# When the input of the next batch is loaded: third group of the batch two ahead, in a cross-attention and expert kernel

## What is computed

```python
def attention(ref_feat, sup_feat):              # ref_feat: layer-normed x, sup_feat: the context
    sup = relu(sup_feat @ W_fc.T + b_fc)
    ref = relu(ref_feat @ W_fc.T + b_fc)
    q = (ref @ W_q.T + b_q).reshape(bs, N1, 16, 16)
    k = (sup @ W_k.T + b_k).reshape(bs, -1, 16, 16)
    p = softmax(einsum('bqhd,bkhd->bhqk', q, k) / 4)
    out_h = einsum('bhqk,bkf->bhqf', p, sup)
    return ref + einsum('bhqf,hjf->bqhj', out_h, Wv).reshape(bs, N1, 256) + b_v

x = x + attention(layernorm(x), ctx)
x = x + ffn(layernorm(x))     # 8 experts, the top 2 of each row, and one base expert
```

## Time and profile before

| | us |
|---|---|
| median of 3 runs | 1425.2 (1423.08 to 1428.62) |
| time of the profiled execution | 1423.38 |
| its span, first to last instruction | 1421.6 |
| TensorE matmul (PE) busy | 1277.0 (90%) |
| TensorE weight load (PEld) busy | 885.3 (62%) |
| VectorE (DVE) busy | 742.6 (52%) |
| ScalarE (ACT) busy | 679.5 (48%) |
| GpSimd (POOL) busy | 240.9 (17%) |

### The profile page before, as it was taken

How to read it: one execution, slowest core, us unless ns; L and a number is a source line. 1 busy time by engine, 2 the same in 40 slices (tenths; PEclk the granted TensorE clock), 3 DMA queues, 4 the chain that set the end, 5 groups by cost and what they waited for, 6 DMA issues and landing times. The chain is left out here.

```text
span 1421.6 us, 24901 instructions
## 1 busy us (share of the span) xinstructions
PE 1277.0 (90%) x8100; PEld 885.3 (62%) x8101; DVE 742.6 (52%) x1550; ACT 679.5 (48%) x938; POOL 240.9 (17%) x236
## 2 busy tenths in 40 slices
PE   4779997997999799799979979999959999999992
PEld 4647775775777577577757757755525556666661
DVE  4246675675667566566756746777435112111113
ACT  4326664664756566466656646665622112222220
POOL 3311110211111111121111102000013601222110
PEclk9879999998999999899989989999979999999996
DMA  4663454455444446444444644453079501111115
GB/s 142 200 174 94 131 138 108 106 154 125 131 117 123 116 114 159 115 131 129 100 116 121 173 112 113 108 106 62 13 222 280 221 26 45 44 44 44 48 45 189
DMA packets 154927, 168.56 MB, mean 119 GB/s; under 512 B 69040, under 2 KB 140344, under 8 KB 154816
## 3 DMA queue, kind: packets, MB, share of 16 engines
q1 hardware_dynamic: 151360, 157.61, 42.1%
q0 software_dynamic: 3456, 9.47, 1.8%
HBM read 103.55 MB, written 63.31 MB: 117 GB/s over the span
## 5 line engine op out<-in xcount | busy, mean ns | idle before, releaser
L602 DVE TENSOR_REDUCE mx<-side 128x1 f32<-128x400 f32 (+1 forms) x1024 | 534.6, 568 | 142.6 <-PE side L454 130.6
L497 ACT ACTIVATE prob<-st 128x1024 f32<-128x1024 f32 (+1 forms) x416 | 411.6, 1022 | 215.8 <-PE st L475 215.4
L454 PE MATMUL side<-kst,qst 96*128 96x400 f32 (+1 forms) x1024 | 330.1, 382 | 3.8 <-DVE mx L602 2.4
L475 PE MATMUL st<-qst,kst 97*128 97x512 f32 (+1 forms) x832 | 268.8, 406 | 35.3 <-issue 28.8
L454 PEld LDWEIGHTS side<-kst,qst 96*128 96x128 f32 x1024 | 189.8, 190 | 115.6 <-issue 37.4
L487 PE MATMUL acc<-prob,v 128*32 128x256 f32 (+1 forms) x3328 | 207.6, 385 | 0.0
L475 PEld LDWEIGHTS st<-qst,kst 97*128 97x128 f32 (+1 forms) x832 | 149.3, 188 | 49.9 <-issue 32.1
L634 POOL TENSOR_TENSOR clo<-raw,chi 128x768 fp32r<-128x768 f32 (+1 forms) x32 | 60.8, 1900 | 517.3 <-ACT chi L528 517.3
L487 PEld LDWEIGHTS acc<-prob,v 128*32 128x32 f32 (+1 forms) x3328 | 95.7, 110 | 79.6 <-issue 23.3
L1432 DVE TENSOR_TENSOR hg<-sg,pu 128x512 f32<-128x512 f32 x40 | 27.5, 688 | 138.4 <-PE pu L1610 138.4
L640 POOL TENSOR_TENSOR flo<-fc,fhi 128x768 fp32r<-128x768 f32 (+1 forms) x32 | 61.0, 1907 | 217.0 <-ACT fhi L541 217.0
(11 more groups left out here) (162 smaller groups left out, 1431.9 us busy)
## 6 DMA issues: line engine op xcount, KB each, us to landing
kst<-parts_at SPq DMA_DIRECT2D x90, 400.2 KB, 5.5
parts_at<-parts SPq DMA_DIRECT2D x48, 384.0 KB, 5.1
v<-v_at SPq DMA_DIRECT2D x32, 408.0 KB
raw<-ctx_t SPq DMA_DIRECT2D x24, 384.0 KB, 3.3
v_at<-vst SPq DMA_DIRECT2D x32, 272.0 KB
wall<-gate_up SPq DMA_DIRECT2D x8, 1024.0 KB, 14.1
parts_at<-parts SPq DMA_DIRECT2D x16, 449.0 KB, 2.8
qst<-q_at SPq DMA_DIRECT2D x192, 32.0 KB, 5.8
```

The costliest lines, as they stand in the source:

```text
L454: pe.matmul(side[u.bank][:, 0:w], t.qst[0:96, pair, col * P:(col + 1) * P], t.kst[0:96, pair, o:o + w], start=True, stop=True).then_inc(si ...
L475: mm = pe.matmul(into[0:rows, i * 2 * NQ:(i + 1) * 2 * NQ], t.kst[0:97, GP * g + i, s * P:s * P + rows], t.qst[0:97, GP * g + i, :], start ...
L497: act.activation(prob[0:rows, s, :], st[(KT * g + s) % 2][0:rows, :], ACT.Exp, scale=float(DH) ** -0.5).then_inc(exp_done, 1)
L602: dve.tensor_reduce(mx[:, hq, r:r + 1], side[u.bank][:, 0:RANGES[r][1]], AX.X, ALU.max)\
```

## The change

`sp_load_x` moves. `x[1]` is now issued once before the batches, behind the last stores of the prologue and ahead of the first row of maxima. In the body, `x[b + 2]` is issued in group 2 of batch `b`, if there is such a batch, in place of `x[b + 1]` in group 0. The wait is now for the `xres` of the same batch's group 1. `x[1]` to `x[7]` are loaded once each, 256 KB a load, before and after the change; `x[0]` is loaded in the setup either way. Nothing else in the program differs.

```diff
                     if c == len(CHUNKS) - 1:
                         sp_load_values(sp, 0, 0)
+                sp_load_x(sp, 1, before_unit(("xres", 0, 0)))
                 sp_max_row(sp, before_unit(("tm", 0, 0)), 0)
 
                 def body(b, at):
...
                             sp_load_group(sp, *behind(b, g, 2))
                         if last + 1 < PHASES:
                             sp_load_values(sp, *behind(b, g, 1))
-                        if g == 0 and at + 1 < B:
-                            sp_load_x(sp, b + 1, resid_unit(b, at))
+                        if g == 2 and at + 2 < B:
+                            sp_load_x(sp, b + 2, body_unit(b, at, 1, "xres", 0))
                         if active(at, g, "p"):
```

## The result

The changed kernel takes 1390.28 us (median of 4 runs, 1389.01 to 1393.02) against 1426.91 us before (1423.08 to 1429.48, 4 runs). The ratio is 0.9748, with a 95% interval of 0.9719 to 0.9777, so it is faster, by 32 to 40 us. The forecast was 1393.5 us in a range of 1387 to 1403. The two profiled executions took 1423.38 and 1393.02 us, 30.4 us apart, which is close to the 31 us of the sum; five more runs in the first experiment give a ratio of 0.9774.

The account below looks back on a forecast made before the run. PE, busy 90% of the span, was taken as the bound, losing time waiting for `xn` and at low clock. Gains of 26.0 + 5.0 = 31 us take 1423.4 to 1392.4; median forecast 1393.5 us, range 1387 to 1403.

Parts of the forecast that it names:

- The load leaves group 0: At batch starts, `x` is in place before VectorE wants it, so PE's waits for `xn` shrink: 26.0 us gained.
- The clock comes back: Behind the long waits in batches 0, 1 and 6, PE no longer runs at half clock: 5.0 us, at most 6.1.
- The jumps back: At the loop's four jumps, PE's remaining waits for `xn` go despite VectorE's own instruction fetch: 2.6 us of the 26.0.
- rival B: VectorE's own way back into the loop holds `xn` at the four jumps: 28 us gained, 1396 us; chance 0.08.
- The load enters group 2: In group 2 the load may hold up key stores by 1 us, against 5.5 us of slack: cost 0.
- The first load: Ahead of the batches, SP has nothing to do between 83.74 and 95.47, so issuing `x[1]` there costs 0.
- what is late next: In group 0, later loads and key stores don't become the bound; shorter PE fetch priced at 0, at most 1 us.
- Rival A: PE's gap closes but other engines set group 0's pace: 12 to 24 us gained, say 1405 us; chance 0.12.
- Rival C: In group 2 the load of `x` delays the new batch's chain, 6.3 us in six batches: 1432 us; chance 0.02.
- Rival D: The load is held up by its wait, or `xn` waits for something else as long: 1425 us; chance 0.03.

Follow-up runs that it names:

- the first experiment: The changed kernel measured again in five rounds against the kernel before: 1392.43 us against 1426.66, ratio 0.9774.
- e4: The kernel before, with PE doing 60 matmuls while it waits for `xn` in batches 0 and 6: 1426.10 us, ratio 0.9998.
- e5: The kernel before with all eight batches written out, so no jump back: 1425.71 us, ratio 0.9968.
- e6: The changed kernel with all eight batches written out, so no jump back: 1357.95 us, ratio 0.9504.
- e3: The kernel before, with the load of `x` kept in group 0 but issued ahead of the group's eleven other loads: 1389.02 us, ratio 0.9751.
- e10: The changed kernel plus two unread 2 MB copies of `x` behind each load of `x` in group 2: 1428.32 us in one run.
- e7: The changed kernel, with SP issuing group 0's stacks and values behind the key stores instead of ahead: 1382.39 us, ratio 0.9680.

## Why the prediction was right

Point by point, by its own steps.

- *The load leaves group 0.* 26.0 us of PE's waits forecast to go, 26.4 gone: 27.0 beyond the prologue before, 0.6 now (14.0 less 13.4). The short wait left over in batch 1 is 0.38 us where I had 0.5.
- *The clock comes back.* The closed gap and the estimate of 6.1 make 9.45 us in batch 0, 9.45 in batch 1 and 10.6 in batch 6. Measured in the groups 0: 9.45, 9.29 and 10.55. Of these 29.3 us some 23.8 are the gaps and 5.5 the clock, halfway between the 5.0 I took and the 6.1. e4 shows the term alone, 1.5 and 2.6 us. What the prediction didn't mention is the half clock behind the four jumps. The change leaves it as it is, so the sum doesn't suffer, but it is some 2 us of each jump's price (e5 and e6).
- *The jumps back.* Forecast 2.6 us, measured 2.1 over four groups, but made up of +0.3, +1.2, -1.5 and -2.1: the fetch itself varies by 1.7 us from jump to jump, so these four can't be told one from another, and that their sum comes so near the forecast is in part luck. What was forecast, the end of the waits for `xn` there, did come: none is left. VectorE was through its own fetch in time at each, so rival B fell; in e3, with a shorter fetch of PE, its mechanism shows with 2.3 us in all. The Trainium skill, Runtime: NRT & Kernel Launch, section Instruction fetch mechanics, says that a taken branch outside the engine's instruction window stalls it until the target has been fetched, and that kernels prefer full unrolling for it. The trace agrees about the stall and gives its length, 6.2 to 7.8 us for PE in the change. Straight code was worth 34 us once `xin` was early (e6), and 2 to 7 us while it was not (e5).
- *The load enters group 2.* Cost 0 forecast, and 0 measured. The load landed in 4.0 us, where I took 5.9 from group 0's crowd, so it doesn't even touch the key stores. I read the slack as 5.5 us, from when the DMA engines fall idle to the first use; but the last to land before that is the raw chunk (issued at 425.27, 4.2 us), which stands behind the stacks. e10 gives 7.3 for the stacks themselves.
- *The first load* and *what is late next*: nothing at either place; no PE wait over 1 us has appeared in groups 0 to 3.
- *Rival A* (others set the pace) fell: the groups 0 lost the gap and the clock's part too, and batch 6's now takes 29.04 us, batch 1's 29.43. *Rival C* (slower, by way of the new batch's stacks) is real as a mechanism and needs two copies of 2 MB, 16 times the load's bytes, to cost what the change gains. *Rival D* (the load isn't really earlier) fell: VectorE's list has no wait for `xin` any more.

In total 31 us were forecast for the profiled execution and 30.3 came. The medians lie 34 to 37 us apart, and 1390.28 is inside the range. Two sums were slightly off: 1392.4 and the 1.8 us to the median make 1394.2, not 1393.5, and rival B's 28 us make 1397, not 1396. Neither matters beside the scatter.

## What to carry to other kernels

A load that is waited for at the head of an in-order engine's loop belongs ahead of the bulk transfers of its queue; the place in the order of one queue was worth as much as two groups of lead. Where a loop's jump and a data wait fall on the same spot, price them together: each alone looked worthless at the jumps (1 to 2 us), both together were 39.5, of which about 8 were the half clock that either of them left behind. And it is worth trying to issue bulk transfers behind the jump rather than across it, for here the engines' own code came in over the same DMA engines (e7).

## What the hardware showed that I had not expected

A jump back stops PE for 6.2 to 8.0 us while SP's loads for the group are under way and for 2.9 to 3.4 us while none is, with the same PE code. It was also shorter, 4.8 to 5.1 us, where `x` was first in the queue (e3), and 4.7 to 5.7 us with PE's code 60 matmuls longer ahead of the loop (e4), though the DMA engines were as full; what sets these last two is open. Each stop is followed by some us at half clock, even the stops of 3 us in e7. The time from issue to landing of the same 256 KB was 5.9 us (median) as the last of the group's loads, 4.0 to 4.5 us in group 2, and 2.9 to 3.1 us as the first (e3).
